# Two residual gates: multiplied into the weights once a batch, or into the result of every tile

## The reference

```python
sa, ca, ga, sb, cb, gb = mod[:, 0], ..., mod[:, 5]          # each (8, 1, 512)
ga = (2 * (ga >= 0) - 1) * jnp.maximum(jnp.abs(ga), 0.25)   # the attention gate
gb = (2 * (gb >= 0) - 1) * jnp.maximum(jnp.abs(gb), 0.25)   # the feed-forward gate
h = _layernorm(x) * (1 + ca) + sa
x = x + ga * attention(h)        # ends in  out @ Wo + bo
h = _layernorm(x) * (1 + cb) + sb
x = x + gb * feed_forward(h)     # base_W and base_b, a shared LoRA, 6 routed LoRAs (top 2)
```

## Time and profile before

| | before |
| --- | --- |
| median of 3 runs | 3259.92 us (3257.35 to 3261.16) |
| the profiled execution | 3262.03 us |
| its span | 3260.2 us |
| mean granted TensorE clock | 0.849 |
| PE busy | 2517.7 us (77%) |
| VectorE busy | 1918.1 us (59%) |
| ScalarE busy | 1451.9 us (45%) |
| GpSimd busy | 796.1 us (24%) |

### The profile page before, as it was taken

How to read it: one execution, slowest core, us unless ns; L and a number is a source line. 1 busy time by engine, 2 the same in 40 slices (tenths; PEclk the granted TensorE clock), 3 DMA queues, 4 the chain that set the end, 5 groups by cost and what they waited for, 6 DMA issues and landing times.

```text
span 3260.2 us, 55786 instructions
## 1 busy us (share of the span) xinstructions
PE 2517.7 (77%) x18184; PEld 1573.5 (48%) x18184; DVE 1918.1 (59%) x4932; ACT 1451.9 (45%) x4829; POOL 796.1 (24%) x708
## 2 busy tenths in 40 slices
PE   5878778678876778877777787777887777886776
PEld 2645555345544555445554455544555455553443
DVE  3545665466654667456664556645666456764665
ACT  1344444354443555344553444534444345543453
POOL 1422232222211322122321222312222222221121
PEclk8978888689897889878888888887888778987887
DMA  5100000100001000000000000000000100000000
GB/s 171 36 4 20 21 17 11 30 14 21 21 7 34 17 14 24 25 13 17 20 17 27 11 20 17 17 27 11 21 21 14 27 17 14 21 17 23 14 17 14
DMA packets 40661, 73.85 MB, mean 23 GB/s; under 512 B 6529, under 2 KB 6529, under 8 KB 40354
## 3 DMA queue, kind: packets, MB, share of 16 engines
q1 hardware_dynamic: 31138, 53.21, 5.3%
q10 hardware_dynamic: 9216, 16.78, 1.4%
HBM read 53.15 MB, written 16.83 MB: 21 GB/s over the span
## 4 chain that ended last, share of the span: by engine, by line
issue 68%; POOL 19%; PE 6%; DVE 3%; ACT 1%; DMA 1%; POOLq 0%; SPq 0%; DVEq 0%; ACTq 0%
POOL csp L1170 5%; POOL css L1162 4%; POOL ra L1154 2%; POOL xc L1183 2%; POOL ra L1188 2%; POOL vec L1150 1%; POOL vea L1146 1%; PE ps_m L484 1%; POOL h_lo L1176 1%; POOL kr L1154 1%; ACT pw L945 1%; PE ps_m L486 1%; PE ps_m L485 1%; DVE ps_s L1387 1%; DMA wb_s<-wb_in 1%
## 5 line engine op out<-in xcount | busy, mean ns | idle before, releaser
L945 ACT ACTIVATE pw<-ps_s,wmax 128x128 f32<-128x128 f32 x1024 | 360.0, 377 | 168.4 <-DVE wmax L1392 168.4
L1413 DVE COPY_PREDICATED pT<-keep_prev,ps_t 128x512 f32<-128x512 uint32 x224 | 163.7, 731 | 453.1 <-PE ps_t L584 443.0
L484 PE MATMUL ps_m<-w_hi,h_hi 128*128 128x512 f32 x768 | 360.7, 470 | 69.5 <-ACT zT L971 31.3
L955 ACT ACTIVATE pw<-pw,wden 128x128 f32<-128x128 f32 x1024 | 313.5, 392 | 91.9 <-DVE wden L1402 86.7
L601 PE MATMUL ps_s<-cst,csp 128*128 128x128 f32 x960 | 192.6, 334 | 177.9 <-POOL csp L1170 143.0
L978 ACT ACTIVATE pT<-ps_s 128x512 f32<-128x512 f32 x240 | 142.1, 592 | 402.0 <-PE ps_s L601 401.7
L485 PE MATMUL ps_m<-w_lo,h_hi 128*128 128x512 f32 x768 | 313.8, 409 | 0.0
L486 PE MATMUL ps_m<-w_hi,h_lo 128*128 128x512 f32 x768 | 313.4, 408 | 0.0
L671 PE MATMUL ps_m<-wbt_s,h2T 128*128 128x512 f32 x512 | 276.3, 631 | 1.5 <-DVE gl L1375 1.5
L1424 DVE TENSOR_REDUCE cm<-css 128x16 f32<-128x256 f32 (+1 forms) x128 | 98.9, 815 | 266.4 <-ACT css L925 266.4
L638 PE MATMUL ps_m<-wo_s,aT 128*128 128x512 f32 x512 | 246.3, 609 | 0.8 <-ACT aT L982 0.8
(11 more groups left out here) (191 smaller groups left out, 4989.2 us busy)
## 6 DMA issues: line engine op xcount, KB each, us to landing
xa<-x_in SPq DMA_DIRECT2D x65, 256.0 KB, 2.7
xc<-x_in SPq DMA_DIRECT2D x64, 256.0 KB, 2.6
out<-t ACTq DMA_DIRECT2D x64, 256.0 KB, 2.0
gbc<-gate_rows SPq DMA_DIRECT2D x24, 256.0 KB, 5.0
pw<-wmod_in SPq DMA_DIRECT2D x3, 1024.0 KB, 5.4
pT<-wmod_in SPq DMA_DIRECT2D x3, 1024.0 KB, 5.2
qT<-wqkv_in SPq DMA_DIRECT2D x2, 1024.0 KB, 8.7
v_s<-wqkv_in SPq DMA_DIRECT2D x1, 1024.0 KB, 11.9
```

Of the source, the lines that this page charges most:

```text
L484: pe_.matmul(ps[:], h_hi[:, c, :], w_hi[:, col, c, :], start=(c == 0), stop=False)
L945: ins = act.activation(pw[:, hw, :], ps_w[:, j, i, 1, :], ACT.Exp, bias=wmax[:, hw:hw + 1], accum_out=wden[:, 0, hw:hw + 1])
L955: act.activation(pw[:, hw, :], pw[:, hw, :], ACT.Copy, scale=wden[:, 2, hw:hw + 1]).then_inc(wn_ok, 1)
```

## The change

Both gates are taken out of the per-tile work and multiplied into the weights. For each batch the unscaled output weights `wo_s` and feed-forward weights `wbt_s` and `wb_s` are loaded again into the same buffers, and GpSimd multiplies their columns with the batch's gate rows (`scale_out`: four instructions of 128x512 in the turn, for the batch to come; `scale_feed`: five in the first slot). VectorE's `residual` and `final` become one addition each, from PSUM and SBUF. SP reloads the output weights once the turn's Y is done and the feed-forward weights once its F is done, and the gates of the next batch are loaded before that, after the turn's `residual_in`. TensorE waits for the scaled weights at tile 0.

```diff
             def load_gates(b):
-                sp.wait_ge(o_ok, NT * b + 1)
+                sp.wait_ge(xb_ok, NT * b + 1)
...
+            def load_out():
+                sp.dma_start(wo_s[:], wo.rearrange("(c p) n -> p c n", p=P)).then_inc(d_wo, 16)
+
+            def load_feed():
+                sp.dma_start(wbt_s[:], wbt.rearrange("(c p) n -> p c n", p=P)).then_inc(d_wf, 16)
+                sp.dma_start(wb_s[:], wb).then_inc(d_wf, 16)
...
+            load_out()
+            load_feed()
             sp.dma_start(wa_s[:], wa.rearrange("(c p) n -> p c n", p=P)).then_inc(d_w, 16)
-            sp.dma_start(wb_s[:], wb).then_inc(d_w, 16)
...
+            load_gates(0)
             def batch(b, a):
-                load_gates(b)
                 load_xc(NT * b, b, 0)
...
                     load_xa(NT * (b + 1) + NT - 2, (b + 2) % B, 0)
+                    load_gates(b + 1)
+                    sp.wait_ge(*m_full_at("loop", b, "Y", NT - 1))
+                    load_out()
+                    sp.wait_ge(*m_full_at("loop", b, "F", NT - 1))
+                    load_feed()
...
-            pe_.wait_ge(d_w, 16 * 4)
+            pe_.wait_ge(d_w, 16)
...
+                    if t == 0:
+                        pe_.wait_ge(wo_ok, NC * (b + 1) + 1)
...
+                    if t == 0:
+                        pe_.wait_ge(wf_ok, (NC + 1) * (b + 1) + 1)
...
-            def store(b, t):
-                act.wait_ge(o_ok, NT * b + t + 2)
+            def store(seg, b, t):
+                act.wait_ge(*m_done_at(seg, b, "F", t))
...
+            def scale_out(b):
+                gp.wait_ge(d_wo, 16 * (b + 1))
+                gp.wait_ge(d_gbc, 16 * (3 * b + 3))
+                for c in range(NC):
+                    gp.tensor_tensor(wo_s[:, c, :], wo_s[:, c, :], gbc[:, 0, :], ALU.mult).then_inc(wo_ok, 1)
+
+            def scale_feed(b):
+                gp.wait_ge(d_wf, 32 * (b + 1))
+                for c in range(NC):
+                    gp.tensor_tensor(wbt_s[:, c, :], wbt_s[:, c, :], gbc[:, 1, :], ALU.mult).then_inc(wf_ok, 1)
+                gp.tensor_tensor(wb_s[:, :], wb_s[:, :], gbc[0:NZ + 1, 1, :], ALU.mult).then_inc(wf_ok, 1)
...
                 residual_in(b, t)
+                scale_feed(b)
                 if a:
                     rotate(seg, b, t, Ta, "K", kr)
...
                 weigh_keys(seg, b, t, Ta)
+                scale_out(ba)
                 deviation_a(Ta + 1)
                 cs_subtract(ba, 0)
...
-                if t == 0:
-                    dve.wait_ge(d_gbc, 16 * (3 * b + 3))
-                dve.wait_ge(o_ok, T + 1)
-                dve.wait_ge(d_out, 16 * (T + 1))
-                dve.tensor_tensor(t1[:], ps[:], gbc[:, 0, :], ALU.mult).then_inc(done, 1)
+                if t:
+                    dve.wait_ge(*m_done_at(seg, b, "F", t - 1))
+                dve.wait_ge(xb_ok, T + 2)
+                dve.tensor_tensor(x1[:], ps[:], xc[:, t % 2, :], ALU.add).then_inc(done, 1)
                 dve.wait_ge(*m_done_at(seg, b, "Y", t))
-                dve.wait_ge(xb_ok, T + 2)
-                dve.tensor_tensor(x1[:], t1[:], xc[:, t % 2, :], ALU.add).then_inc(y_ok, 1)
-                dve.wait_ge(y_ok, T + 2)
                 ln_stats(x1[:], stc, mvc, vec, lnc, T)
...
-                dve.tensor_tensor(t1[:], ps[:], gbc[:, 1, :], ALU.mult).then_inc(done, 1)
-                dve.wait_ge(*m_done_at(seg, b, "F", t))
-                dve.tensor_tensor(t1[:], x1[:], t1[:], ALU.add).then_inc(o_ok, 1)
+                dve.wait_ge(d_out, 16 * (T + 1))
+                dve.tensor_tensor(t1[:], ps[:], x1[:], ALU.add).then_inc(done, 1)
```

More of the change, by code:

```diff
@@ L273, in program @@
         d_w = sem("d_w")
+        d_wo, d_wf = sem("d_wo"), sem("d_wf")
         d_mod = [sem("d_mod0"), sem("d_mod1")]
@@ L311, in program @@
         xb_ok = sem("xb_ok")
-        y_ok = sem("y_ok")
+        wo_ok, wf_ok = sem("wo_ok"), sem("wf_ok")
         r_ok, r_exp = sem("r_ok"), sem("r_exp")
-        o_ok = sem("o_ok")
         modc_ok, moda_ok = sem("modc_ok"), sem("moda_ok")
@@ L320, in program @@
                     wmax_ok, wn_ok, cs_ok, cs_exp, cs_shift, cs_norm, lna, lnc, lnap, lncp, rope_ok, qsum_ok, g_ok, g_exp,
-                    c_full, c_done, ckp_ok, ckr_ok, b_ok, xb_ok, y_ok, r_ok, r_exp, o_ok, modc_ok, moda_ok,
+                    c_full, c_done, ckp_ok, ckr_ok, b_ok, xb_ok, wo_ok, wf_ok, r_ok, r_exp, modc_ok, moda_ok,
                     whi_ok, wlo_ok, hhi_ok, hlo_ok)
@@ L405, in _ @@
                 load_mod(i)
-            sp.dma_start(wo_s[:], wo.rearrange("(c p) n -> p c n", p=P)).then_inc(d_w, 16)
-            sp.dma_start(wbt_s[:], wbt.rearrange("(c p) n -> p c n", p=P)).then_inc(d_w, 16)
+            load_out()
+            load_feed()
             sp.dma_start(wa_s[:], wa.rearrange("(c p) n -> p c n", p=P)).then_inc(d_w, 16)
-            sp.dma_start(wb_s[:], wb).then_inc(d_w, 16)
             sp.wait_ge(set_v, GUARD_STEPS + 1)
@@ L1028, in first_slot @@
                     copy_v(seg, b, t)
-                store(b, t)
+                store(seg, b, t)
             def slot(seg, b, s):
```

## The result

The changed kernel takes 3207.76 us (median of 4 runs, 3205.02 to 3212.32), the kernel before 3260.54 us beside it (4 runs): a ratio of 0.9835, 95% interval 0.9812 to 0.9858. It is 53 us faster; 30 were forecast. The profiled execution has a span of 3203.2 us, 57.0 us less than before.

The account below looks back on a forecast made before the run. Up to the Q transposes' end a middle slot was bounded by VectorE's list, then by TensorE's. Savings of 42 x 1.64 + 8 + 1.4 = 78 us, less 48 for the clock, left 30: 3230 us, range 3178 to 3264.

Parts of the forecast that it names:

- The stall: Middle slots: the old addition waits 1.6 us behind GpSimd's `css`; the new one would not, 1.64 us saved a slot.
- The bound of 2.26: Middle slots: upper limit of the saving in us a slot, if ScalarE's part moves earlier too.
- The other places: Outside the looped middle slots: first slots 8 us in seven batches, kernel's end 1.4, turns and last batch's middle slots 0.
- The end: Kernel's end: both removed instructions lie on the path, 0.72 us each, 1.4 saved.
- What it adds: Turn and first slot: nine GpSimd multiplications a batch, about 1.28 us each, 92 us in eight batches, all hidden.
- The clock: Middle slots: TensorE's clock rises early or late, deciding on 3.7 us a slot; it takes back 48 of 78 us.
- 18 late ones: Middle slots, of 42, whose clock was forecast to rise late; 13 more than now, at 3.7 us each.
- the loop's end: TensorE's 6.72 us idle there: might move with the transfers by 2 us either way, 14 in seven batches; taken as 0.
- the rival in which the clock takes nothing: Middle slots: early rises stay the rule, all 78 us remain, 3182 us; with partial forms, 3178 to 3215, chance 0.25.
- a hidden stall: Middle slots: the stall was hidden anyway, or about 24 to 28 slots are late; 3253 to 3266 us, chance 0.13.
- a clock late nearly everywhere: Middle slots: the clock rises late in nearly all; with all 42 late 59 us slower, 3319 us, chance 0.10.
- GpSimd's work coming through: Turn and first slot: GpSimd's added multiplications cost their full 92 us; 14 us slower, 3274 us, chance 0.02.

Follow-up runs that it names:

- the padded kernels: Changed kernel and kernel before, each with matmuls on zeros in TensorE's idle stretches of middle slots, holding the clock there at 1.00: 3057.45 and 3152.71 us.

## Why the prediction came out as it did

**The stall.** Right in mechanism and size. 1.64 us a middle slot were forecast; the idle stretch shrank by 1.70, and at a held clock the slots by 1.67, 70.1 us in 42 against the 69 of the sum. L1431 waits for ScalarE, as L1400 was to; it starts 0.04 us after ScalarE's end, where 0.1 had been allowed. The bound of 2.26 did not come.

**The other places.** First slots 1.2 us each forecast, 8 in seven; 7.1 measured, 7.9 between the padded kernels. That the sum fits so well is luck in part: five of the seven went from about 38.5 to 36.9 us, 1.6 each, one from 37.5, and the last from 35.0 to 36.9 us, so it became longer. The end 1.4 forecast and 1.4 measured: from the start of the last output projection to the last store it is 20.25 us before and 18.85 after. The last batch's middle slots 0 forecast, 1.3 slower measured.

**What it adds.** GpSimd's multiplications at 1.28 forecast and hidden: four of `wo_s` take 5.12 us, and leaving all nine out changes nothing. Charged in full, by the rival, the work would have made the kernel 14 us slower. Its busy time of 883 us was forecast near 890. No stall behind them shows in the time.

**The clock.** The forecast had it take back 48 us, with slots of two kinds at 42.8 and 46.6 us. Measured: two kinds at 42.6 to 43.1 and 46.3 to 46.5, and 47.8 us taken back. The count behind it was less exact: 18 late ones were forecast, and there are 14 at 46.4, with seven more (the last of each six, a slot with fewer instructions) at 43.7 where they were 42.6. The mechanism is as forecast; that 48 met 47.8 is luck in part.

**The step that was mis-sized** is the loop's end. The text saw 6.72 us of idleness without a releaser, named the fetch of instructions as a candidate and that it may move with the transfers, gave it 2 us either way a batch, a size behind which stood no row, and took 0. It measured 3.5 us less in each of six turns (41.0 to 20.0 us). All seven turns gained 25.6 us: TensorE's busy time in them fell by 7 us with it (462.8 to 455.8), while the seventh, which has no loop end, became 2.7 us longer. With 25 in place of 0 the sum would be 30 + 25 = 55; 53 were measured. The reason for taking 0 was that two megabytes stand at the turn where one and a half did; what counts by the runs is what is under way when the engine reaches its loop end, and there the gates are gone.

So the time of 3208 us lies in the range, but below the forecast's own 3215 to 3253, in the band that was given to the rival in which the clock takes nothing. That rival is refuted all the same: the clock took its part. The rivals of a hidden stall, of a clock late nearly everywhere, and of GpSimd's work coming through are refuted as well.

## What to carry to other kernels

Where an instruction of VectorE with two SBUF inputs takes longer in some places than in others, look at what GpSimd runs beside it, and let one of its inputs come from PSUM. Before a gain or a loss of a microsecond in a repeated stretch is priced, see whether TensorE's granted clock is below 1.00 there: the clock can swallow it, and filling TensorE's idle stretches (150 us here) may be worth more than the edit, and shows what the edit is worth. Look at every engine's idle time at the back edge of a loop, and try to move large transfers that are under way when an engine reaches it; the trace has to show that the entry shrinks, since it did not follow the issue times alone here.

## What was unexpected of the hardware

Work on the critical chain can be free: 42 memsets of 1.34 us changed the time by nothing that could be measured, while the same ones cost 70 us once the clock was held. A single test in which added work costs nothing is no proof of room.

At the loop's back edge TensorE and VectorE stand idle for some microseconds on `issue`: some 3 to 4.6 us where the gates' loads were moved away (TensorE 19.0 to 25.6 us in six, VectorE 19.2), and up to 8 us where loads were issued just ahead (TensorE 41.0 in six in the kernel before, VectorE 35.3 with the three loads put back). The trace of the kernel before shows one packet of one instruction queue, and two of another, among 755 of data in that stretch:

```profile
q1 hardware_dynamic: 611, 1.09, 60.5%
q10 hardware_dynamic: 144, 0.26, 10.1%
q8 instruction: 1, 0.02, 1.0%
```

(queue, kind: packets, MB, share of 16 engines, from 1381 to 1388 us). That the engines' next instructions come through the same DMA engines and stand behind that data fits TensorE's entry in every kernel here in which the loads were moved or kept, but it is inferred from the times; no run shows the queueing itself. One row stands against a simple rule: VectorE reaches its end at 1362.47 us in the changed kernel with the DMA engines busy for the most part, and its stretch is 3.87 us. How much traffic it takes, and at which moment, stays open. Why the first six turns of the kernel before differ among each other (87.9 to 95.7 us, where those of the changed kernel take 87.0 to 87.3) stays open beyond the clock's part.
